# A fused attention and expert kernel on one Trainium2 core: a projection half a step sooner, its parts fetched as a step opens

## The reference

```python
def attn(x):                     # x: 16 x 256 x 128, 16 heads of width 8, causal
    Q, K, V = einsum(x, WQ), einsum(x, WK), einsum(x, WV)
    scores = where(causal, Q @ K.T / sqrt(8), -inf)
    return concat_heads(softmax(scores) @ V) @ WO
def ffn(x):                      # 8 experts, hidden width 512
    aff = x @ centroids.T
    e = argmax(aff); alpha = sigmoid(aff[e])
    h = relu(layernorm(x, ln_g[e], ln_b[e]) @ w1[e].T + b1[e])
    return alpha * (x + h @ w2[e].T + b2[e]) + (1 - alpha) * x
x = x + layernorm(attn(layernorm(x)))
x = x + layernorm(ffn(layernorm(x)))
```

## Time and profile before

| | |
|---|---|
| timed runs | 455.62, 449.07, 454.79 us (median 454.79) |
| profiled execution | 450.13 us, its span 448.2 us |
| busy share of the span | PE 77%, DVE 75%, PEld 61%, ACT 55%, POOL 54% |
| attention part | to about 330 us |
| mean granted clock of TensorE | 0.922 of full speed |
| DMA | 42.81 MB, mean 96 GB/s; queue q1 43.1% of the 16 engines' span |

### The profile page before, as it was taken

One profiled execution on the slowest core, in us unless ns is written; L12 is line 12 of the kernel. 1 busy time (PEld: TensorE's weight loads), 2 busy tenths in 40 slices (PEclk: granted clock), 3 DMA queues, 4 the chain that ended last, 5 costly groups with the idle time before them and its releaser, 6 DMA issues.

```text
span 448.2 us, 11647 instructions
## 1 busy us (share of the span) xinstructions
PE 342.9 (77%) x3642; PEld 272.2 (61%) x3642; DVE 338.2 (75%) x1215; ACT 244.3 (55%) x574; POOL 242.7 (54%) x337
## 2 busy tenths in 40 slices
PE   2358798798898897898798967987307799899960
PEld 1136576576676675676576755754206788788860
DVE  7848786777988986988958949676452788888980
ACT  2204466567576575577566644564105577777750
POOL 3913255444566566476556555566540366666773
PEclk9998999999999998999989969898556999999995
DMA  7661854744553552553633627020044566666710
GB/s 208 110 103 45 142 88 78 100 86 84 76 92 75 77 102 49 86 94 65 91 81 47 102 58 97 14 84 16 19 118 106 135 172 168 158 168 171 191 55 6
DMA packets 34684, 42.81 MB, mean 96 GB/s; under 512 B 5465, under 2 KB 25053, under 8 KB 33088
## 3 DMA queue, kind: packets, MB, share of 16 engines
q1 hardware_dynamic: 31744, 37.43, 43.1%
q0 software_dynamic: 2304, 4.37, 3.0%
q10 hardware_dynamic: 576, 0.27, 0.2%
HBM read 30.59 MB, written 11.66 MB: 94 GB/s over the span
## 4 chain that ended last, share of the span: by engine, by line
PE 38%; DMA 26%; DVE 11%; SPq 9%; issue 7%; POOL 6%; ACT 1%; POOLq 0%; DVEq 0%
DMA aug<-nmT 20%; PE ST L838 5%; PE O L859 4%; PE S L825 4%; DVE nmf L1100 3%; PE S L1006 3%; PE S L818 2%; PE S L815 2%; SPq L377 2%; PE S L820 2%; SPq L373 2%; PE MB L1019 2%; PE ST L847 2%; DMA aug<-qk_parts 2%; PE O L1019 2%
## 5 line engine op out<-in xcount | busy, mean ns | idle before, releaser
L1100 DVE TENSOR_REDUCE nmf<-S 128x2 f32<-128x512 f32 (+1 forms) x192 | 129.9, 682 | 51.9 <-PE S L818 24.8
L431 POOL TENSOR_SCALAR_AFFINE_SELECT p<-p 128x512 f32<-128x512 f32 x64 | 40.8, 638 | 81.3 <-ACT p L598 81.1
L598 ACT ACTIVATE p<-ST 128x1024 f32<-128x1024 f32 x64 | 65.4, 1021 | 23.1 <-PE ST L838 22.4
L838 PE MATMUL ST<-aug 128*128 128x256 bf16 x256 | 40.1, 281 | 28.4 <-DMA aug<-nmT 28.4
L825 PE MATMUL S<-aug 126*128 126x128 bf16 x512 | 51.7, 225 | 0.0
L461 POOL DMA_INDIRECT xs_rows<-pay,pos x32 | 33.0, 1033 | 28.8 <-DVE pos L1259 25.0
L529 POOL DMA_INDIRECT out_x<-vaug,x_all x39 | 40.8, 1045 | 7.9 <-issue 6.3
L435 POOL TENSOR_SCALAR_AFFINE_SELECT p<-p 128x512 f32<-128x512 f32 x64 | 41.4, 647 | 6.3 <-ACT p L602 3.4
L539 POOL TENSOR_TENSOR rsz<-vez,mhalf 128x1 f32<-128x1 f32 x39 | 22.1, 566 | 39.8 <-DVE vez L1452 39.7
L838 PEld LDWEIGHTS ST<-aug 128*128 128x128 bf16 x256 | 23.3, 99 | 33.4 <-DMA aug<-nmT 30.8
L825 PEld LDWEIGHTS S<-aug 126*128 126x128 bf16 x512 | 41.2, 101 | 2.5
(11 more groups left out here) (163 smaller groups left out, 867.5 us busy)
## 6 DMA issues: line engine op xcount, KB each, us to landing
w1s<-in_w1x SPq DMA_DIRECT2D x39, 259.0 KB
qk_parts<-qkp SPq DMA_DIRECT2D x16, 384.0 KB, 2.8
aug<-qk_parts SPq DMA_DIRECT2D x32, 192.0 KB
aug<-qk_parts SPq DMA_DIRECT2D x32, 128.0 KB
x_all<-xs_rows SPq DMA_DIRECT2D x39, 67.0 KB, 2.5
aug<-qk_parts SPq DMA_DIRECT2D x32, 64.0 KB
w_tab<-in_w2t SPq DMA_DIRECT2D x8, 256.0 KB, 6.5
out_x<-vaug,x_all POOLq DMA_INDIRECT x39, 3.1
```

The lines of the kernel that those rows point to most:

```text
L431: g.affine_select(out=v, in_=v, compare_op=ALU.is_ge, fill=0.0, base=0, pattern=[[0, 4], [1, P]], channel_multiplier=-1).then_inc(s["sel0" ...
L598: a.activation(p0[:, gr % 2], ST0[:, :, :], ACT.Exp, scale=SCALE).then_inc(s["exp0"], 1)
L838: last = mm(ST0[:, j], kaug[:, p, h, 0:P], qaug[:, p, h], start=True, stop=True)
L1100: v.tensor_reduce(dst, S[:, n % 2].rearrange("p (j n) -> p j n", j=k), op=ALU.max, axis=AX_X, negate=True).then_inc(s["red"], 1)
```

## The change

On all engines the order of calls within a step changes; no operation is added or removed. `project_qk(i + 3)` moves on PE from group 3 to group 2, behind `scores_near` and the first unit of `scores_by_query`, and `high`, `residue`, `middle`, `low` move with it: `residue` to ahead of the maxima of group 3, `middle` to ahead of `exp_near` of group 3, `low` to ahead of `select` of group 3. `normalise_x` is made a step sooner, at the end of a step. On SP `parts_out` of batch i + 3 is the last of step i, and `parts_in` of batch i + 2 is the first, ahead of both `shift`s. `transpose_o`, `affinities_and_ranks`, `transpose_x`, `project_v` (PE), `alphas`, `place`, `divide`, `choose`, `count` (DVE), `scatter`, `power`, `number` (POOL), `affinities_and_ranks_out`, `v_out` (ACT) change places.

```diff
 # SP, ahead of the steps
             shift(Nth(0), 0)
+            parts_out(Nth(2))
 
             def step(i):
+                if b := at(i, 2):
+                    parts_in(b)
                 if b := at(i, 0):
                     shift(b, 1)
-                if b := at(i, 2):
-                    parts_out(b)
-                if b := at(i, 2):
-                    parts_in(b)
                 if b := at(i, 1):
                     shift(b, 0)
+                if b := at(i, 3):
+                    parts_out(b)
...
 # POOL
+                if last:
+                    scatter(last, 0)
+                if new:
+                    low(new)
                 if t:
                     select(t, 3)
...
 # ACT
                 if t:
+                    exp_far(t, 1)
                     exp_near(t, 2)
...
+                if nxt:
+                    shift_out(nxt, 0)
+                if new:
+                    high(new)
                 if t:
                     exp_far(t, 2)
...
+                if new:
+                    middle(new)
                 if t:
                     exp_near(t, 3)
                 if old:
                     onT_out(old)
+                if nxt:
+                    v_out(nxt)
                 if t:
                     exp_far(t, 3)
-                if new:
-                    high(new)
                 if ln:
                     exp_negative(ln)
-                if new:
-                    middle(new)
+                if b := at(i, 4):
+                    normalise_x(b)
...
 # PE
+                    if gr == 2 and nxt:
+                        transpose_shift(nxt, 0)
+                    if gr == 2 and new:
+                        project_qk(new)
...
+                    if gr == 1 and new:
+                        transpose_x(new)
...
-                    if gr == 2 and nxt:
-                        transpose_shift(nxt, 0)
-                    if gr == 3 and new:
-                        project_qk(new)
+                    if gr == 1 and old:
+                        transpose_o(old)
...
-                    if gr == 2 and nxt:
+                    if gr == 3 and nxt:
                         project_v(nxt)
...
 # DVE
                 if l2:
                     ln_variance(l2, 1)
+                if new:
+                    residue(new)
                 if nxt:
                     maxima_and_stats(i, nxt, 3, 0)
...
                 if nxt:
                     maxima_and_stats(i, nxt, 3, 2)
-                if new:
-                    residue(new)
```

More of the change, by code:

```diff
@@ L499, in step @@
             def step(i):
-                t, ln, last = at(i, 0), at(i, -2), at(i, -4)
+                t, new, ln, last = at(i, 0), at(i, 3), at(i, -2), at(i, -4)
                 if t:
@@ L510, in step @@
                 if last:
-                    scatter(last, 0)
+                    scatter(last, 1)
                 if ln:
                     power(ln, 1)
-                if last:
-                    scatter(last, 1)
-                if ln:
                     number(ln)
@@ L519, in step @@
                     power_x(i.k + 3)
-                if b := at(i, 3):
-                    low(b)
             iterations(pool, step)
@@ L661, in _ @@
             middle(Nth(2))
+            normalise_x(Nth(RING))
             def step(i):
@@ L673, in step @@
                     o_out(old)
-                if new:
-                    normalise_x(new)
                 if ln:
@@ L679, in step @@
                     exp_near(t, 1)
-                    exp_far(t, 1)
+                if ln or last:
+                    affinities_and_ranks_out(i.plus(-3), ln, last)
                 if new:
@@ L683, in step @@
                 if t:
+                    exp_far(t, 1)
                     exp_near(t, 2)
-                if ln or last:
-                    affinities_and_ranks_out(i.plus(-3), ln, last)
+                if nxt:
+                    shift_out(nxt, 0)
+                if new:
+                    high(new)
                 if t:
                     exp_far(t, 2)
[L689 to L692, removed]
+                if new:
+                    middle(new)
                 if t:
@@ L951, in step @@
                         project_o(l2)
-                    if gr == 1 and old:
-                        transpose_o(old)
-                    if gr == 2 and i.k == 1:
+                    if gr == 1 and i.k == 1:
                         centroid_sums()
-                    if gr == 2 and (ln or last):
+                    if gr == 1 and (ln or last):
                         affinities_and_ranks(i.plus(-3), ln, last)
+                    if gr == 2 and nxt:
+                        transpose_shift(nxt, 0)
+                    if gr == 2 and new:
+                        project_qk(new)
                     if gr == 3 and old:
@@ L971, in step @@
                         weigh_values(t, gr - 1)
-                    if gr == 2 and nxt:
-                        transpose_shift(nxt, 0)
-                    if gr == 3 and new:
-                        project_qk(new)
+                    if gr == 1 and old:
+                        transpose_o(old)
                     if nxt:
                         scores_by_query(nxt, gr, 2)
-                    if gr == 1 and new:
-                        transpose_x(new)
-                    if gr == 2 and nxt:
+                    if gr == 3 and nxt:
                         project_v(nxt)
@@ L1297, in step @@
                     maxima_and_stats(i, nxt, 0, 0)
-                if nxt:
                     maxima_and_stats(i, nxt, 0, 1)
@@ L1309, in step @@
                     maxima_and_stats(i, nxt, 1, 0)
+                if l4:
+                    alphas(l4, 0)
                 if nxt:
@@ L1314, in step @@
                 if l4:
-                    alphas(l4, 0)
+                    alphas(l4, 1)
+                if i.k == 1:
+                    centre_centroids()
+                if nxt:
+                    maxima_and_stats(i, nxt, 1, 2)
+                if l4:
+                    place(l4, 0)
+                if nxt:
+                    shift_parts(nxt, 0)
                 if old:
                     divide(old)
[L1318 to L1321, removed]
                 if nxt:
                     maxima_and_stats(i, nxt, 2, 0)
-                    shift_parts(nxt, 0)
+                if l4:
+                    place(l4, 1)
+                if l3:
+                    choose(l3, 0)
                 if l2:
                     add_y(l2)
+                if l4:
+                    place(l4, 2)
                 if nxt:
@@ L1330, in step @@
                     ln_stats(l2, 1)
[L1331 to L1334, removed]
                 if l3:
-                    choose(l3, 0)
+                    choose(l3, 1)
                     ln_shift(l3)
@@ L1341, in step @@
                     maxima_and_stats(i, nxt, 2, 2)
-                if l4:
-                    place(l4, 1)
                 if l3:
-                    choose(l3, 1)
                     scale_max(l3)
@@ L1348, in step @@
                     ln_variance(l2, 1)
+                if new:
+                    residue(new)
                 if nxt:
                     maxima_and_stats(i, nxt, 3, 0)
-                if l4:
-                    place(l4, 2)
                 if l3:
@@ L1360, in step @@
                     maxima_and_stats(i, nxt, 3, 2)
-                if new:
-                    residue(new)
+                if l3:
+                    count(l3, 0)
                 if nxt:
@@ L1365, in step @@
                 if l3:
-                    count(l3, 0)
                     count(l3, 1)
```

## The result

| | before | changed |
|---|---|---|
| timed runs, median | 453.63 us (449.07 to 455.62) | 536.31 us (533.35 to 539.07) |
| profiled execution's span | 448.2 us | 534.2 us |
| TensorE, busy / mean granted clock | 77% / 0.922 | 69% / 0.866 |
| queue q1, share of the 16 engines' span | 43.1% | 35.3% |

The ratio is 1.195, with a 95% interval of 1.189 to 1.200: the changed kernel is 19.5% slower. It was predicted as 539 us, slower.

What follows compares the result with a forecast made beforehand. Bound: DMA of row maxima held behind parts_in. New loop 8.6 + 2.8 + 10.4 = 21.8, plus 1.6 slow clock, 23.4 us; 53 + 13 x 23.4 + 2 = 359, 89 later; 450 + 89 = 539 us, range 495 to 562.

Steps and rivals of the forecast that it cites:

- The loop and its place: Attention steps: scores_near waits for half 1 about 14 times, at group 2 not group 0, 4 to 7 us each.
- B: VectorE reaches the residue as soon as high is done, so parts are ready early; 18.6 us a loop, 477 us; chance 0.07.
- C: Half 1 isn't held by parts_in's data, only issued late; no change within 2%, 446 to 462 us; chance 0.07.
- D: Half 1 isn't held and VectorE keeps up, parts_out landing before the step ends; 419 us; chance 0.04.
- Rival A: TensorE's clock stays full through the new stalls; 21.8 us a loop, 518 us; chance 0.25.
- X to parts_out: From group 2's start through projection, high, residue, middle and low: 8.6 us, plus 1.6 for the slow clock.
- X: Start of scores_near of group 2 in a step; forecast at 53 in step 0 and 359 in step 13.
- parts_out to parts_in: SyncE's queue: 2.8 us for the write to land before parts_in's first transfer is issued.
- parts_in to X: From parts_in's first issue until half 1 lands behind its data and group 2 starts: 10.4 us.
- The rule of the Trainium skill on completion out of order: DMA transfers needn't complete in issue order, so half 1 could overtake parts_in; spoke against the forecast.
- The 2 us for the weight tables: Steps 0 to 3 issue weight tables behind parts_out, ahead of parts_in: 2 us in all, between nothing and 4.
- Covered edits: Reordered calls on ACT, DVE and PE cost nothing, covered by 5 us slack; uncovered, divide would hold project_qk about 0.7 us.

Runs made afterwards that it cites:

- the kernel of 429 us: The changed kernel with one edit in SyncE's queue: half 1 of the maxima issued ahead of parts_in; 429.21 us, 0.949 to before.

## Why the prediction was right, step by step

- *The loop and its place.* As predicted: 14 waits of scores_near, all at group 2, none at group 0 that a transfer causes. In length 5.0 to 7.9 us, the forecast said 4 to 7. Rivals B, C and D are out: no half 1 lands early, and parts_out leaves 9.0 to 10.4 us behind group 2's start. Rival A is out too: behind all 14 stalls the granted clock reads 0.50 in the first three us of group 2.
- *X to parts_out.* Forecast 8.6 + 1.6 = 10.2; measured in the 13 steps 9.0 to 10.4, mean 9.9 (299.87 - 289.68 = 10.2 above). The path is the forecast's: the residue comes behind VectorE's queue, 7.6 us after X (297.25), against 6.1 + 1.6 = 7.7. That the sum fits is luck, though, since its two terms are off in opposite ways. With the clock up, parts_out leaves at X + 7.9 and not 8.6, as the experiment with the matmuls in the stall shows: from the second maxima to the residue VectorE needs 2.4 us, where the sum took 3.35 from another stretch of the kernel before. And the slow clock costs 2.1 us in the mean (9.94 - 7.87), not 1.6. At full clock the loop is 20.9 us, so rival A's 21.8 was too long as well.
- *parts_out to parts_in.* This term was mis-sized: 2.8 us, from the earlier trace rows; measured 2.8 to 4.6, mean 3.45 over 13 steps, so 8 us in all. The page gives a median of 3.2 us from issue to landing, 2.8 before. The trace says what goes with the slow ones: a packet of 8 or 16 KB in a queue of the kind "instruction" while the parts are being written. The DMA queues during the slowest, from 347.77 to 352.38 us:

```profile
q1 hardware_dynamic: 784, 0.39, 31.0%
q0 software_dynamic: 32, 0.07, 5.4%
q8 instruction: 1, 0.02, 2.4%
```

and during a quick one, from 181.38 to 184.13 us:

```profile
q1 hardware_dynamic: 784, 0.39, 50.2%
```

All six of the 13 that took over 3.3 us (3.5 to 4.6) have such a packet between their issue and their landing, and so has the one of 4.3 us in the kernel before (246.45 to 250.77). In the traces of before, the changed kernel and four experiments, 84 writes, none without such a packet took over 3.1 us; some with one were quick too (2.75). No experiment was made on it, so the cause is read from the rows and not shown.
- *parts_in to X.* Forecast 10.4, measured 9.7 to 12.0 over 14, mean 10.4. The sentence on what holds half 1 was too loose: "its data for theirs" is right, "with nothing ahead" in its queue isn't the point. The DMA engines' load holds it, in whatever queue it stands.
- *The rule of the Trainium skill on completion out of order* (DMA: Bandwidth & Descriptors, "Queues, rings and completion order"), as the prediction took it, would have given 446 to 462 us. It doesn't show: 14 of 14 in this kernel and 14 of 14 on a queue of its own landed behind parts_in. The prediction used half of that section. It states too that one DMA engine marks a transfer as complete only after all of that engine's earlier writes, across its queues, which would hold half 1 wherever the two transfers share engines; which engines they use, no run shows.
- *Sum.* The loop is 23.85 instead of 23.4 us: parts_out to parts_in +0.65, X to parts_out -0.26, parts_in to X +0.07. Step 0's X was 52.56 (53 forecast), step 13's 362.61 (359). The 2 us for the weight tables don't show: the four steps that have them take 23.7 us in the mean, the nine others 23.9. What follows was forecast as unchanged and takes 171.6 us instead of 178.2 (534.2 - 362.61, and 448.2 - 270.03), 6.6 us less; the cause of that is open. The errors cancel in part: the total, 539 forecast and 536.31 measured, is closer than its terms.
- *Covered edits.* divide and transpose_o do cost, once the slack of the stall is gone (what place and alphas cost wasn't read): in the kernel of 429 us project_qk waits 0.42 us for divide (0.7 was the bound), VectorE 0.88 us for scores behind transpose_o. In the changed kernel the first wait doesn't show, and the second is there but lies ahead of the stall and costs nothing.

## What to carry to other kernels

A small transfer that the next matmuls wait for should be issued ahead of a large one that shares the DMA engines (another issuer's queue was no way round that here), and the time to count runs from the first issue of the large one. When a prefetch is moved ahead, ask which small transfers it overtakes, and whether what it fetches is itself made behind the wait for one of them: then write and read latency together become the step's length. A long stall of TensorE costs more than its own length, here 2 us behind one of 6. And a sum that fits should be tested term by term: here two terms between group 2's start and parts_out were off by 0.7 and 0.5 us and hid one another.

## What was not expected of the hardware

- An 8 KB transfer on ScalarE's queue, which held nothing else, took 7.1 us beside a 768 KB one on SyncE's, and ended when it would have ended behind it; beside a quarter of that, in the same queue, it took 2.0 us.
- Reading the data back by quarter-length rows (2 KB instead of 8 KB) made the stretch from the first issue to the end of half 1 4.4 us long, of which 2.35 us are issues: 6 us less for 576 KB less.
- parts_out (384 KB to DRAM) took from 2.8 to 4.6 us until parts_in could be issued, in steps of one kernel that look alike; in the kernel before it was 2.8 us in the middle, once 4.3. The long ones have a packet of an instruction queue in their time.
